# A selective scan whose drives move from GpSimd to TensorE, with turned operands and diagonals

## The reference

```python
u = conv4(layernorm(x)) + conv_b                  # 4 taps over positions
dt, Bm, Cm = split(u @ xproj_w.T, [128, 16, 16])
delta = softplus(dt @ dtproj_w.T + dtproj_b)      # [b, t, d]
deltaA  = exp(delta[..., None] * A)               # decay, 16 states
deltaBu = delta[..., None] * Bm[:, :, None, :] * u[..., None]   # drive
h = deltaA[t] * h + deltaBu[t]                    # over t, per (d, state)
y[t] = sum over states of h * Cm[t]
x = x + y + u * D_skip
```

## Time and profile before

| what | value |
| --- | --- |
| median of 3 runs | 221.69 us (221.39 to 223.66) |
| span of the profiled execution | 221.1 us |
| busy: TensorE | 161.8 us (73%) |
| busy: VectorE | 194.2 us (88%) |
| busy: ScalarE | 159.4 us (72%) |
| busy: GpSimd | 148.7 us (67%) |

### The profile page before, as it was taken

How to read it: one execution, slowest core, us unless ns; L and a number is a source line. 1 busy time by engine, 2 the same in 40 slices (tenths; PEclk the granted TensorE clock), 3 DMA queues, 4 the chain that set the end, 5 groups by cost and what they waited for, 6 DMA issues and landing times.

```text
span 221.1 us, 3460 instructions
## 1 busy us (share of the span) xinstructions
PE 161.8 (73%) x952; PEld 111.6 (50%) x952; DVE 194.2 (88%) x401; ACT 159.4 (72%) x353; POOL 148.7 (67%) x150
## 2 busy tenths in 40 slices
PE   8379698887962865983586756667696968676789
PEld 3145385565651753753485545455564555443344
DVE  1789987999899999999989999997999979886663
ACT  3549979879799976956795757874777896773251
POOL 2510379999999899999999899886426363434000
PEclk9958999999998599999969996997999999999999
DMA  5993951854543633546333651510000000000203
GB/s 159 327 365 98 186 185 37 212 139 138 166 158 110 179 113 102 187 77 187 112 100 98 162 125 44 203 42 0 0 0 1 3 0 0 0 3 27 71 0 98
DMA packets 15109, 23.29 MB, mean 105 GB/s; under 512 B 1137, under 2 KB 6641, under 8 KB 15089
## 3 DMA queue, kind: packets, MB, share of 16 engines
q1 hardware_dynamic: 13792, 21.92, 35.0%
q10 hardware_dynamic: 1296, 1.15, 1.6%
HBM read 21.88 MB, written 1.18 MB: 104 GB/s over the span
## 4 chain that ended last, share of the span: by engine, by line
DVE 35%; PE 20%; issue 18%; ACT 15%; POOL 8%; DMA 1%; ACTq 1%; POOLq 0%; DVEq 0%
DVE hid L1108 9%; DVE hid_sb L1108 6%; DVE prod L1119 5%; POOL drive L348 4%; ACT pD L494 4%; PE pY L986 3%; PE pF L918 3%; PE pY L786 3%; DVE w L1294 2%; DVE am L1053 2%; PE pA L253 2%; POOL prod L385 2%; ACT w L591 1%; DMA x_sb<-x 1%; ACT L494 1%
## 5 line engine op out<-in xcount | busy, mean ns | idle before, releaser
L348 POOL TENSOR_TENSOR drive<-du,bc 128x512 f32<-128x512 f32 x64 | 79.9, 1277 | 4.3 <-DMA bc<-bc_dram 4.1
L494 ACT ACTIVATE pD<-delta,negA 128x255 f32<-128x255 f32 x128 | 54.9, 468 | 15.1 <-DVE hid L1108 12.8
L1108 DVE TENSOR_TENSOR_SCAN hid<-pD,drive 128x512 f32<-128x512 f32 x40 | 48.9, 1223 | 3.1 <-ACT pD L494 1.4
L786 PE MATMUL pY<-ident,prod 128*128 128x128 f32 x256 | 36.8, 294 | 14.0 <-POOL prod L385 10.7
L986 PE MATMUL pY<-zero 128*128 128x512 bf16 x148 | 41.0, 402 | 1.0 <-POOL zero L305 1.0
L786 PEld LDWEIGHTS pY<-ident,prod 128*128 128x128 f32 x256 | 31.2, 152 | 19.9 <-DVE prod L1119 10.2
L385 POOL TENSOR_TENSOR prod<-hid_sb,bc 128x512 f32<-128x512 f32 x24 | 30.5, 1278 | 2.3 <-DVE hid_sb L1108 2.2
L1108 DVE TENSOR_TENSOR_SCAN hid_sb<-pD,drive 128x512 f32<-128x512 f32 x24 | 29.0, 1207 | 0.9 <-ACT pD L494 0.9
L1119 DVE TENSOR_TENSOR prod<-hid,bc 128x512 f32<-128x512 f32 x40 | 27.1, 679 | 0.5 <-PE pY L786 0.2
L333 POOL TENSOR_TENSOR rstd<-ve,mhalf 128x2 f32<-128x2 f32 x12 | 8.6, 715 | 24.5 <-ACT ve L678 24.5
L986 PEld LDWEIGHTS pY<-zero 128*128 128x128 bf16 x148 | 14.9, 103 | 12.6 <-issue 2.7
(11 more groups left out here) (166 smaller groups left out, 328.2 us busy)
## 6 DMA issues: line engine op xcount, KB each, us to landing
bc<-bc_dram SPq DMA_DIRECT2D x32, 512.0 KB, 4.9
w<-w_gate_up SPq DMA_DIRECT2D x1, 1408.0 KB, 8.5
x_sb<-x SPq DMA_DIRECT2D x4, 256.0 KB, 3.6
fs_t<-w_in_t SPq DMA_DIRECT2D x1, 1024.0 KB, 11.8
out<-x_sb ACTq DMA_DIRECT2D x8, 128.0 KB, 2.3
w<-w_down SPq DMA_DIRECT2D x1, 704.0 KB, 9.8
ctx_t<-w_out_t SPq DMA_DIRECT2D x1, 512.0 KB, 11.7
xproj<-xproj_t SPq DMA_DIRECT2D x1, 160.0 KB, 3.0
```

What stands on the lines that cost most here:

```text
L348: pool.tensor_tensor(drive[:, s % 2, h], du[:, b, h].unsqueeze(1).to_broadcast([P, SPS, T]), bc[:, g % 4, 0].rearrange("p (n t) -> p n t", ...
L494: act.activation(decay[:, h, n, 1:T], delta[:, b, h, 1:T], ACT.Exp, scale=negA[:, h, k:k + 1]).then_inc(S["decay_ready"], 1)
L786: ins = pe.matmul(pY[:, j, h * P:(h + 1) * P], prod[:, s % 2, h, n, j * P:(j + 1) * P], ident[:], start=(s + n + h + j == 0), stop=False, ...
L1108: dve.tensor_tensor_scan(hid_sb[:, k % 2] if pooled(s, h) else hid, decay[:, h].rearrange("p n t -> p (n t)"), drive[:, s % 2, h].rearrang ...
```

## The change

- **Drives.** 56 of the 64 are now made by TensorE. Once a batch du is turned by TensorE (turn_du) and copied to SBUF by ScalarE (out_du), and B's columns (bt) come from four small matmuls in prep_bc and a copy on VectorE. For each step GpSimd spreads B's columns on diagonals (diagonal: affine_select, 128x512, two buffers), and drive_turned multiplies: du_t is loaded as weights, the diagonal streams, two f32 matmuls of 128x256 a half step. The result lies in PSUM, in one of two state banks, and the scan runs on it in place. The other eight (half 1 of the odd steps of batches 0 and 1) stay on GpSimd.
- **Weighs.** GpSimd has 48 (half 1, and both halves of odd steps), VectorE 16.
- **Decays.** Those of turned half steps go to a ring of four in SBUF (decay_sb); those of the eight others to one PSUM bank.
- **Loads.** C's rows come alone, 256 KB a step; B's rows only for the eight plain drives.
- **Orders.** All lists are rewritten. Fillers go from 148 matmuls to 114, of which 8 stand among the scans of batches 2 and 3 and none among those of batches 0 and 1; 28 stand ahead of the first transposes (14 before) and 26 near the end (22 before). Several maxima of VectorE move from before the first scan into batch 0, some of the expert's work between batches and from the tail to before the last scans. Some pairs of semaphores are merged.

Core of the diff (orders left out):

```diff
-        def pooled(s, h):
+        def pooled(g, h):
-            return h == 1 and s % 4 != 3
+            return h == 1 or g % 2 == 1
...
+        def turned(g, h):
+            return h == 0 or g % 2 == 0 or g >= 16
...
+            def diagonal(b, s):
+                g = STEPS * b + s
+                pool.wait_ge(S["bt_out"], b + 1)
                 if g >= 2:
+                    pool.wait_ge(S["driven_ready"], driven(g - 1, 0))
+                pool.affine_select(out=diag[:, g % 2].rearrange("p n j t -> p (n j) t"),
+                                   in_=bt[:, b, SPS * s:SPS * (s + 1)].rearrange("p n j -> p (n j)").unsqueeze(2).to_broadcast([P, SPS * JT, P]),
+                                   compare_op=ALU.is_equal, fill=0.0, base=0, pattern=[[0, SPS * JT], [-1, P]],
+                                   channel_multiplier=1).then_inc(S["diag_made"], 1)
...
+                if turned(g, h):
+                    k = driven(g, h)
+                    to = decay_sb[:, k % 4]
+                    if k >= 4:
+                        act.wait_ge(S["scanned"], scans_to(k - 4, True))
...
+            def out_du(b):
+                act.wait_ge(S["du_turned"], b + 1)
+                act.activation(du_t[:, b].rearrange("p j d -> p (j d)"), conv_bank(b), ACT.Copy).then_inc(S["du_t_out"], 1)
...
+            def drive_turned(b, s, h):
+                g = STEPS * b + s
+                k = driven(g, h)
+                pe.wait_ge(S["du_t_out"], b + 1)
+                pe.wait_ge(S["diag_made"], g + 1)
+                if k >= 2:
+                    pe.wait_ge(S["scanned"], scans_to(k - 2, True))
+                    pe.wait_ge(S["weighed0"], weighs_to(k - 2))
+                to = state[k % 2].rearrange("p (n t) -> p n t", n=SPS)
+                for j in range(JT):
+                    ins = pe.matmul(to[:, :, j * P:(j + 1) * P], du_t[:, b, j, h * P:(h + 1) * P], diag[:, g % 2, :, j],
+                                    start=(j == 0), stop=(j == JT - 1), skip_group_check=True)
+                ins.then_inc(S["driven_ready"], 1)
...
+                if turned(g, h):
+                    k = driven(g, h)
+                    dve.wait_ge(S["driven_ready"], k + 1)
+                    by, add = decay_sb[:, k % 4], state[k % 2]
```

More of the change, by code:

```diff
@@ L409, in _ @@
-            weigh(3, 6, 1); residual2(1); multiply3(0, 0); rsqrt(1, 3); smooth2(2); rsqrt(2, 1); multiply3(0, 1)
-            smooth1(3); multiply3(1, 0); residual2(2); multiply3(1, 1); final(0, 0); rsqrt(2, 2); smooth2(3)
-            final(0, 1); final(1, 0); multiply3(2, 0); multiply3(2, 1); final(1, 1); rsqrt(2, 3); final(2, 0)
-            final(2, 1)
+            pads(); constants(); rsqrt(0, 0); diagonals(1); rsqrt(0, 1); rsqrt(0, 2); diagonal(0, 0); diagonal(0, 1)
+            drive_step(0, 1, 1); drive_step(0, 3, 1); diagonal(0, 2); weigh(0, 0, 1); rsqrt(0, 3); weigh(0, 1, 0)
@@ L415, in _ @@
+            weigh(3, 6, 1); residual2(1); multiply3(0, 0); weigh(3, 7, 0); weigh(3, 7, 1); rsqrt(2, 1); rsqrt(1, 3)
+            smooth2(2); multiply3(0, 1); smooth1(3); multiply3(1, 0); residual2(2); multiply3(1, 1); rsqrt(2, 2)
+            final(0, 0); smooth2(3); multiply3(2, 0); final(0, 1); multiply3(2, 1); final(1, 0); final(1, 1)
+            final(2, 0); final(2, 1); rsqrt(2, 3)
         @block.scalar
@@ L1022, in _ @@
+            mm3(3, 1, 0); mm3(3, 1, 1); filler(5, 13); turn_qf(3, 0); turn_qf(3, 1); mm4(3, 0); mm4(3, 1)
         @block.vector
@@ new lines, in _ @@
+            scan(2, 6, 1); inv_smooth1(1); scan(2, 7, 0); expert_out(0); scan(2, 7, 1); scan(3, 0, 0); stats3(0)
+            max_w(1); scan(3, 0, 1); max_x(1); weigh(3, 0, 0); scale_x1(1); max3(0); inv_x1(1); scale_w1(1)
+            residual1(2); inv_w1(1); scan(3, 1, 0); scan(3, 1, 1); stats2(2); scan(3, 2, 0); scan(3, 2, 1)
+            weigh(3, 2, 0); gate_up1(1); scale3(0); gate1(1); inv3(0); scan(3, 3, 0); up1(1); shift(1, 2); amax_a(1)
+            scan(3, 3, 1); ratio_a(1); scan(3, 4, 0); inv_smooth2(1); amax_x(2); weigh(3, 4, 0); scan(3, 4, 1)
@@ new lines, in _ @@
+            max_ad(1); gate_up3(0, 0, 0); scale_ad(1); ratio_x(2); inv_ad(1); scan(3, 5, 0); scan(3, 5, 1)
+            gate_up3(0, 0, 1); inv_smooth1(2); scan(3, 6, 0); scan(3, 6, 1); expert_out(1); max_w(2); weigh(3, 6, 0)
+            scale_w1(2); max_x(2); full3(0); scale_x1(2); inv_w1(2); stats3(1); inv_x1(2); scan(3, 7, 0)
+            scan(3, 7, 1); gate_up3(0, 1, 0); max4(0, 0); max3(1); gate_up3(0, 1, 1); scale3(1); gate_up1(2)
+            inv3(1); residual1(3); stats2(3); up1(2); scale4(0, 0); amax_a(2); full3(1); ratio_a(2); inv4(0, 0)
```

419 lines of the change are left out of this document (221 added, 198 removed), and 1 row of the table names.

## The result

The changed kernel takes 215.39 us (median of four runs, 215.07 to 215.67). The kernel before, run beside it, took 222.68 (221.39 to 223.82; its runs fall around 221.5 and 223.7, so a ratio to it moves by some tenths of a per cent with the runs that it is set against). The ratio is 0.970, with a 95% interval of 0.966 to 0.974: 3.0% faster. The profiled execution has a span of 213.8 us, 7.3 less than before, where 3.8 less were forecast.

What follows compares the result with a forecast made beforehand. ScalarE's list was to limit batches 0 and 1, VectorE's batches 2 and 3. Span 221.1 + 0 to scan(2,0,0) - 1.9 in batches 2 and 3 - 1.9 in the tail = 217.3, plus 0.6: 217.9 us, range 211.5 to 225.5.

Steps and rivals of the forecast that it cites:

- VectorE's 8 us of batches 0 and 1: Batches 0 and 1: VectorE's 8 us become idle time because ScalarE's list is full; net 0 up to scan(2,0,0).
- the prediction's sign: Batches 0 and 1: if right, VectorE's idle time is up by several us, waiting for ScalarE's decays.
- the first scan: Head: the first decay moves from 25.96 to 24.2 us and the first scan to 26.8.
- The term for the longer filler: Head: 14 more matmuls in the first filler cost 2.3 us; TensorE's dt and pre gain an estimated 0.8.
- +1.5 for waits on TensorE: Batches 2 and 3: VectorE waits 1.5 us on TensorE, charged within the 67.4 us forecast there.
- the tail: After the last scan: the tail was forecast to get 1.9 us shorter.
- -3.3 + 1.9 = -1.4: Tail: VectorE loses 3.3 us of moved work and a weigh; the weighs of (3,7), both on GpSimd, add 1.9.
- The forecast's 1.1: Tail: x3q waited 1.83 us behind stores; moving two stores earlier was to give back 1.1.
- the diagonal: GpSimd: a 128x512 affine_select was taken as 0.89 us, the middle of 0.59 to 1.18.
- TensorE as the bound: Batches 2 and 3: rival in which TensorE's waits and clock make the kernel slower, 225.5 us; chance 0.20.
- the point of decision: Batches 2 and 3: the TensorE rival decides from 72.4 us of TensorE's work and waits, 223.9 in all.
- Rival 1: Whole recurrence: VectorE's saving is kept whole, scan(2,0,0) at 84.2, then 65.9 us, 211.9 in all; chance 0.17.

Runs made afterwards that it cites:

- ln_together: The changed kernel with the logarithms of batches 2 and 3 side by side again, two table loads fewer on ScalarE: 212.75 us.
- Ring3: The changed kernel with three buffers, not four, in the ring of decays in SBUF: 229.81 us.
- stores_back: The changed kernel with two output stores, (0,1) and (1,0), again between quant3(3) and unmagic3(3): 215.65 us.
- half_sum: The changed kernel with TensorE making 4 of each step's 8 transposes into the sum, the second state of each pair left out of y: 214.63 us.
- filler14: The changed kernel with 14 matmuls in the first filler, as in the kernel before, not 28: 213.71 us.

## Why the prediction was right, and where it missed

**Right: direction, range, and where the gain would not be.** The range held 215.4, 2.5 us below the 217.9 forecast; the gain in span, 7.3 us, is nearly twice the 3.8 forecast. The argument that decided it was that VectorE's 8 us of batches 0 and 1 would be lost to a full ScalarE. It held, and for batch 1 ln_together shows it by taking two of ScalarE's loads away. For batch 0 it is read from the windows alone (28.4 of 28.7 us), since no run changed ScalarE's work there. That scan(2,0,0) came out to the tenth is luck, for three errors cancelled: ScalarE's list was 60.1 us, not 62.0, and waited 2.8, not 1.6, from a first decay at 24.9, not 24.2. VectorE's idle time in batches 0 and 1 grew from 4.2 to 9.1 us, but its longest piece, the 3.45, waits for a logarithm, where the prediction's sign named decays.

**Missed: the first scan, 28.0 and not 26.8.** I charged the turned du to ScalarE and TensorE as work, and forgot that it is a chain: du, its transpose, its copy, the drive. The first scan waited 0.52 us for that drive with its decay ready. The term for the longer filler, 2.3 - 0.8 = 1.5, was of the right size: the first scan comes at 25.3 to 26.0 in the three kernels with the short one and at 26.5 to 28.0 with the long one.

**Missed: "+1.5 for waits on TensorE" in batches 2 and 3.** This is the largest error. VectorE's work there was 63.8, forecast 67.4 - 4.0 = 63.4; its idle time did not grow from 2.5 to 4.0 but shrank to 1.2. A TensorE with 62 of 65 us of work made VectorE wait hardly at all. That two state banks let drives run ahead is a likely reason; no run varied them. Ring3 shows another: without the fourth decay buffer, in an order written for four, batches 2 and 3 take 75.2 us. So ScalarE's running ahead did more than the prediction allowed it.

**Mis-sized: the tail, -3.1 and not -1.9.** From the last scan's end to the start of the last quantising of y it fell from 43.9 to 41.9 us, where -3.3 + 1.9 = -1.4 stood; from there to the end from 19.2 to 18.1. The forecast's 1.1 stands in the second part, but the two stores are not what gave it (stores_back). A third, of the output (0,0), stood there too before; that was not tried, and the cause stays open.

**Off, with no effect: the diagonal,** 0.64 where 0.89 was taken, near the lower end of 0.59 to 1.18. GpSimd had room in any case: 48.4 us of 65.05 in batches 2 and 3.

**The rivals.** TensorE as the bound fell with half_sum, although it became nearly as full as VectorE; the point of decision, 72.4 us of its work and waits, was far off, with batches 2 and 3 at 65.05. The price of that rival was also too high by its own rows: 68.8 / 0.93 = 74.0 slows down old work that was measured at 0.93 already. With the drives alone slowed it is 37.5 + 2.4 + 28.8 / 0.93 = 70.9, so 3.1 us less, and the range's upper end should have stood near 222.4. Rival 1 held for batches 2 and 3 (65.05 against its 65.9) and failed where ScalarE stood. On the clock: the prediction says that transposes and f32 drives do what a filler does, but its rows hold transposes only the earlier trace rows. The changed kernel, with 8 filler matmuls among its scans, ran them at 1.00 in the profiled execution, transposes and drives mixed. That does not test what the Trainium skill, page "TensorE: Matmul & The Clock Gate", Part 4, says of transposes, since drives run among them; the rows of the kernel before remain what speaks against it.

## What to carry to other kernels

Work taken from the fullest engine pays in a stage only as far as the next list there is shorter: compare each engine's list with the stage's length, for every stage. A chain of waits that names one engine for two thirds of the span may only say that this engine never rests; take work away from it, and put work on the others, before believing it. Where an edit may move the clock, compare executions at the same granted clock, or the fall is counted as the edit's effect. In lists executed in order, the depth of a ring decides how much unrelated work a wait holds up, and an instruction that is moved forward delays whoever waits for what it passed.

## What the runs showed of the hardware

- A 128x512 affine_select on GpSimd took 0.64 us, a 128x128 one 0.295: by these two, an estimated 0.11 for each further 128 columns.
- A 128x255 activation on ScalarE took 0.498 us into SBUF and 0.464 into PSUM, with the same operands in one kernel.
- What a wait does to the clock is not fixed: after the same 2.6 us wait of TensorE it stayed at 1.00 in the change's profiled execution and fell to 0.52 in filler14's, with the same instructions there. The fall cost batch 1 0.8 us.
- The opening fillers ran at the lower level (0.43 us from one start to the next, then 0.22) for a length that differed from one execution to the next: 28 of them took 7.6 to 9.1 us, and the first scan moved with it.
